# Two elementwise products of the finishing stage go from VectorE to Pool

## The reference

```
# attention: o per head (4 heads of 32), RMS norm per token and head, output product
o = o * rsqrt(mean(o * o, axis=-1) + 1e-5) * rms_w
o = o.reshape(B, L, 128) @ Wo
# feed-forward, 352 hidden columns, blocks of 16 rounded to FP4 with a scale each
gate = fp4_linear(x, w_gate);  y = fp4_linear(x, w_up)
h = silu(gate) * y
x + o + fp4_linear(h, w_down)
```

## Time and profile before

| | |
|---|---|
| median of 3 runs | 1819.68 us (1816.97 to 1820.57) |
| profiled execution | span 1818.1 us; no other time of it is shown |
| VectorE busy, share of the span | 1475.4 us, 81% |
| TensorE busy | 1450.2 us, 80% |
| ScalarE busy | 1025.9 us, 56% |
| Pool busy | 20.0 us, 1% |
| finishing pass | from 1553.3 us to the end, 16 tiles |

### The profile page before, as it was taken

The page is one execution under the profiler, slowest core; times in us unless marked ns, Lnnn a source line. Parts: engine busy times, 40 slices in busy tenths (PEclk is TensorE's granted clock), DMA queues, the critical chain, the costliest instruction groups (busy, mean ns, idle before and its releaser), DMA issues. The chain is left out here.

```text
span 1818.1 us, 38591 instructions
## 1 busy us (share of the span) xinstructions
PE 1450.2 (80%) x13559; PEld 1057.3 (58%) x13559; DVE 1475.4 (81%) x3537; ACT 1025.9 (56%) x1764; POOL 20.0 (1%) x41
## 2 busy tenths in 40 slices
PE   1569989999999999999977878724666567677776
PEld 0546666666666666666655666513555555466665
DVE  6785139888888888888877999859888887599996
ACT  0564348777777777777766777601111111577774
POOL 3000000000000000000000000000000000000000
PEclk9779999999999999999998899965556655788887
DMA  7000000000000000000001222250332210111111
GB/s 210 0 0 1 1 0 1 1 1 1 0 0 0 0 0 0 0 0 0 1 1 41 87 103 99 87 151 6 91 86 62 62 50 16 49 54 53 53 49 33
DMA packets 80860, 65.76 MB, mean 36 GB/s; under 512 B 3680, under 2 KB 65504, under 8 KB 80736
## 3 DMA queue, kind: packets, MB, share of 16 engines
q1 hardware_dynamic: 70128, 58.26, 10.3%
q10 hardware_dynamic: 10608, 5.79, 1.1%
HBM read 34.68 MB, written 29.36 MB: 35 GB/s over the span
## 5 line engine op out<-in xcount | busy, mean ns | idle before, releaser
L911 ACT ACTIVATE glu_a<-moe_a,b1s 128x512 f32<-128x512 f32 x256 | 176.7, 690 | 130.6 <-PE moe_a L822 128.3
L916 ACT ACTIVATE b_raw<-moe_b,b1s 128x512 f32<-128x512 f32 x256 | 176.3, 689 | 0.7 <-PE moe_b L822 0.5
L968 DVE TENSOR_TENSOR glu_a<-glu_a,moe_g 128x512 f32<-128x512 f32 x256 | 175.8, 687 | 0.0
L975 DVE TENSOR_TENSOR h_lo<-glu_a,h_hi 128x512 fp32r<-128x512 f32 x256 | 175.3, 685 | 0.6 <-ACT h_hi L927 0.6
L960 DVE SCALAR_TENSOR_TENSOR glu_a<-glu_a,b_raw 128x512 f32<-128x512 f32 x256 | 175.3, 685 | 0.1
L927 ACT ACTIVATE h_hi<-glu_a 128x512 fp32r<-128x512 f32 x256 | 161.8, 632 | 18.6 <-DVE glu_a L968 3.2
L951 DVE TENSOR_SCALAR b_raw<-b_raw 128x512 f32<-128x512 f32 x256 | 108.9, 425 | 72.9 <-ACT b_raw L916 72.9
L820 PE MATMUL moe_a<-x_hi,w_hi 128*128 128x512 f32 x256 | 127.2, 497 | 2.8 <-DVE w_lo L987 2.8
L849 PE MATMUL moe_y<-h_hi,w_hi 128*128 128x512 f32 x256 | 102.0, 399 | 2.7 <-DVE h_lo L975 2.7
L820 PE MATMUL moe_b<-x_hi,w_hi 128*128 128x512 f32 x256 | 101.7, 397 | 0.0
L821 PE MATMUL moe_a<-x_lo,w_hi 128*128 128x512 f32 x256 | 101.2, 395 | 0.0
(11 more groups left out here) (269 smaller groups left out, 3304.5 us busy)
## 6 DMA issues: line engine op xcount, KB each, us to landing
kq_scratch<-kq_out SPq DMA_DIRECT2D x16, 512.0 KB, 3.2
kq_in<-kq_scratch SPq DMA_DIRECT2D x16, 512.0 KB, 5.0
acc<-in_L_attn_inputs SPq DMA_DIRECT2D x8, 512.0 KB, 10.1
xq_scratch<-qT SPq DMA_DIRECT2D x16, 256.0 KB, 2.0
v_scratch<-v_out SPq DMA_DIRECT2D x16, 256.0 KB, 2.0
k_scratch<-k_out SPq DMA_DIRECT2D x16, 256.0 KB, 2.3
k_in<-k_scratch SPq DMA_DIRECT2D x8, 512.0 KB, 7.7
v_in<-v_scratch SPq DMA_DIRECT2D x8, 512.0 KB, 7.5
```

Of the source, the lines that this page charges most:

```text
L911: act.activation(glu_a[e % 4][:, :], ps_a[u][:, :], ACT.Gelu_apprx_sigmoid, bias=w["b1"][:, 0, e:e + 1]).then_inc(a_glu, 1)
L916: act.activation(b_raw[u][:, :], ps_b[u][:, :], ACT.Identity, bias=w["b1"][:, 1, e:e + 1])\
L968: dve.tensor_tensor(a, a, ps_g[u][:, :], ALU.mult).then_inc(weighted, 1)
L975: dve.tensor_tensor(h_lo[e % 2][:, :], glu_a[e % 4][:, :], h_hi[e % 2][:, :], ALU.subtract)\
```

## The change

`join` and `divide_o` are issued by Pool instead of VectorE, in a sweep of Pool's own, with the same operands. A new semaphore `divided` counts the second. VectorE's chain semaphore `o_chain` counts two steps per tile instead of three. In VectorE's list `back_o` moves from ahead of the first `add_h` to behind the second.

```diff
--- before.py
+++ after.py
@@ -1712,7 +1712,7 @@
         h_scaled, h_sized, h_over, c_set = sem("h_scaled"), sem("h_sized"), sem("h_over_ready"), sem("c_set")
         h_chain, h_ready, h_turned, h_copied = sem("h_chain"), sem("h_ready"), sem("h_turned"), sem("h_copied")
         down, final, stored = sem("ffn_down"), sem("final"), [sem(f"fin_stored{i}") for i in range(2)]
-        round_chain = sem("h_round_chain")
+        round_chain, divided = sem("h_round_chain"), sem("o_divided")
         acc = w["acc"]
 
         def half(a, h):
@@ -1726,6 +1726,21 @@
             @block.gpsimd
             def _(pool):
                 pool.memset(minus_c[:, :], -FP4_SHIFT * FP4_ONE).then_inc(c_set, 1)
+
+                def join(t, u):
+                    wait_free(pool, h_turned, t, 3)
+                    pool.wait_ge(silued, SUBS * (t + 1))
+                    pool.wait_ge(up_copied, SUBS * (t + 1))
+                    pool.tensor_tensor(hid[u][:, :, :], gated[u][:, :, :], lifted[u][:, :, :], ALU.mult)\
+                        .then_inc(joined, 1)
+
+                def divide_o(t, u):
+                    pool.wait_ge(o_chain, 2 * t + 2)
+                    r = rows[:, :].rearrange("p (n d) -> p n d", d=HD)
+                    pool.tensor_tensor(r, r, inv[:, :].unsqueeze(2).to_broadcast([P, NT, HD]), ALU.mult)\
+                        .then_inc(divided, 1)
+
+                sweep(pool, TILES, [(1, join), (1, divide_o)])
 
             @block.sync
             def _(sp):
@@ -1838,32 +1853,17 @@
 
                 def mean_o(t, u):
 
-                    dve.wait_ge(o_chain, 3 * t + 1)
+                    dve.wait_ge(o_chain, 2 * t + 1)
                     dve.tensor_scalar(m2[:, :], m2[:, :], 1.0 / HD, EPS, ALU.mult, ALU.add).then_inc(m2_ready, 1)
 
                 def invert_o(t, u):
                     dve.wait_ge(rooted, t + 1)
                     dve.reciprocal(inv[:, :], root[:, :]).then_inc(o_chain, 1)
 
-                def divide_o(t, u):
-                    dve.wait_ge(o_chain, 3 * t + 2)
-                    r = rows[:, :].rearrange("p (n d) -> p n d", d=HD)
-                    dve.tensor_tensor(r, r, inv[:, :].unsqueeze(2).to_broadcast([P, NT, HD]), ALU.mult)\
-                       .then_inc(o_chain, 1)
-
                 def back_o(t, u):
-                    dve.wait_ge(o_chain, 3 * t + 3)
+                    dve.wait_ge(divided, t + 1)
                     wait_free(dve, down, t, 1)
                     dve.transpose(oN[u][:, :], rows[:, :]).then_inc(o_ready, 1)
-
-                def join(t, u):
-                    wait_free(dve, h_turned, t, 3)
-                    dve.wait_ge(silued, SUBS * (t + 1))
-                    dve.wait_ge(up_copied, SUBS * (t + 1))
-                    dve.tensor_tensor(hid[u][:, :, :], gated[u][:, :, :], lifted[u][:, :, :], ALU.mult)\
-                       .then_inc(joined, 1)
-
-
 
                 groups = "p j (g k) -> p j g k"
                 spread = lambda a, h: a.rearrange("p (j g) -> p j g", j=SUBS)[:, 2 * h:2 * h + 2, :].unsqueeze(3)\
@@ -1927,9 +1927,9 @@
                                       ALU.add).then_inc(final, 1)
 
 
-                sweep(dve, TILES, [(1, turn_o), (1, join), (1, sum_o), (1, max_h), (1, mean_o), (1, scale_h),
+                sweep(dve, TILES, [(1, turn_o), (1, sum_o), (1, max_h), (1, mean_o), (1, scale_h),
                                    (1, invert_h), (1, divide_h(0)), (1, divide_h(1)), (1, negate_h),
-                                   (1, invert_o), (1, divide_o), (1, back_o), (1, add_h(0)), (2, finish), (1, add_h(1)),
+                                   (1, invert_o), (1, add_h(0)), (2, finish), (1, add_h(1)), (1, back_o),
                                    (1, subtract_h(0)), (1, subtract_h(1)), (1, multiply_h(0)), (1, multiply_h(1))])
```

## The result

The changed kernel takes 1875.78 us (median of 4 runs, 1873.71 to 1876.34) against 1820.12 us for the kernel before: 55.7 us more, ratio 1.0302 with a 95% interval of 1.0288 to 1.0317. It is slower, as forecast, but by five times the 10.9 us of the sum. The time is near that of rival A (1883 us), which had a chance of 0.32.

The account below looks back on a forecast made before the run. The prediction took the chain from multiply_h through TensorE, ScalarE and the second h_over to VectorE as the bound. It summed 10.1 + 1.3 - 0.5 = +10.9 us on 1819.7 to 1831 us (own range 1824 to 1836); full range 1824 to 1888.

Parts of the forecast that it names:

- the sum: Whole kernel: back_o 10.1, first tile 1.3, less 0.5 for join leaving VectorE, +10.9 us in all.
- rival A: VectorE's burst ending the step: Pool's join shuts out two-tile instructions, 3.5 us a step, 1883 us; chance 0.32.
- The chain bounds the step, VectorE's total doesn't: Each step: multiply_h, transposes, ScalarE, second h_over take 11.09 us, then VectorE alone 4.10 us.
- back_o on the chain, 16 x 0.63 = 10.1 us: Between second add_h and first subtract_h: back_o costs 0.63 us at each of 16 tiles, at most 11.4 in all.
- divide_o, gain 0: Ahead of VectorE's wait for h_over: its 0.69 us only lengthens the wait; on Pool 0.7, 1.3 or 2.1 us.
- First tile, +1.3: First tile, where ScalarE waits for mean_o: a join of 3.5 us on Pool delays max_h, +1.3 us.
- join leaves VectorE, gain 0.5 us: Start of step: mean_o comes 0.7 us earlier, but the root rarely waited for it; 0.5 us gained over the stage.
- So join may take 15.82 + 3.08 - 13.03 = 5.87 us at no price: From last lifted to next step's max_h: a join on Pool up to 5.87 us long costs nothing.
- All three are hidden: Pool's join at each estimated length, 1.58, 3.5 or 5.7 us, fits its room, the top by 0.2 us only.
- Rival B: VectorE's burst keeps Pool's join out until the step's end; max_h 0.5 us late, 1838 us; chance 0.18.
- Slower, 0.89: Whole kernel: chance of being slower by more than about 4 us, mostly needing only back_o on the chain.
- The steps of before lie between 14.8 and 15.4: Steps of the kernel before, in us; cited for TensorE's clock perhaps moving the forecast by 2 us.

Follow-up runs that it names:

- a1: Kernel before with only back_o moved behind the second add_h, join and divide_o staying on VectorE: 1831.88 us against 1821.95.
- a4: Changed kernel with one more wait, so Pool's join starts only when the tile before is multiplied: 1837.48 us, +15.5 against the kernel before.
- a3: Kernel before with only join moved to Pool: 1869.14 us, ratio 1.0268.
- c1: Kernel before with VectorE's order alone changed and each store a step later, nothing on Pool: 1812.70 us against 1820.16.
- c3: c1 with invert_o ahead of scale_h and TensorE's turn_h in two halves: 1804.53 us against 1820.16 for the kernel before.
- a2: Kernel before with only divide_o moved to Pool, back_o in its old place: 1822.60 us, ratio 1.0009.
- c2: c3 with divide_o on Pool, released by invert_o: 1801.66 us against 1820.16 for the kernel before.
- c4: c2 with the first half of join on Pool too, released when the tile before is multiplied: 1796.91 us against 1820.16 for the kernel before.
- b2: Kernel before plus, per tile on Pool, a 128x1408 copy behind a one-element-a-row product, nothing waiting for it: 1838.69 us against 1820.88.

## Why the prediction was wrong, point by point

- *The chain bounds the step, VectorE's total doesn't*: right. a1 moves one instruction and pays 9.9 us; the wait for h_over swallowed what left VectorE (41.2 us of it after, 40 predicted).
- *back_o on the chain, 16 x 0.63 = 10.1 us*: right, 9.9 in a1.
- *divide_o, gain 0*: right, +0.65 with an interval across zero; its length of 1.05 us lay between the bounds.
- *First tile, +1.3*: 1.1.
- *join leaves VectorE, gain 0.5 us*: no run isolates it; it is within the noise.
- *"So join may take 15.82 + 3.08 - 13.03 = 5.87 us at no price", and "All three are hidden"*: this step failed. It asked only who waits for join, and by that measure it was right (a4 shows the room: a max_h that starts 0.3 us beyond it costs 0.3). It left out what no row of before shows: that Pool's instruction, while it reads SBUF, holds off a VectorE instruction with two inputs in SBUF. The term was put at 0 and measured 3.04 us a step, +47.2 us in a3. It stood in rival A with the right place (the burst behind the second add_h), the right condition and a price of 3.5 us a step, against 3.04. I gave it 0.32 because no row showed Pool reading beside a two-tile instruction. But no row excluded it either. The absence of such a row was no evidence for a price of 0, and the timing, the worst possible, was known.
- *Rival B* (Pool is kept out until the burst ends): false. Pool came in at the first boundary between two VectorE instructions, in the middle of the burst.
- *The range, 1824 to 1888*: 1875.78 lies in it only because rival A had been taken into it. The forecast's own range ended at 1836. *Slower, 0.89*: back_o alone makes the kernel slower by an amount clear of noise, so the direction rested on a mechanism that holds; five sixths of the loss came from the one that was left out of the sum.
- *"The steps of before lie between 14.8 and 15.4"*: two of them are 14.74 us. Nothing hangs on it.

## What to carry to other kernels

Before an operation is moved to Pool, look at what VectorE does at the time when its inputs are complete. If VectorE's instructions there read two SBUF tiles and lie on the chain, they are late by nearly the length of Pool's instruction (here 2.95 us for 3.16), though no semaphore says so. Release it where VectorE waits or reads one tile (a4: one wait, some 40 us). And VectorE, busy for 94% of a step, wasn't the step's bound, since it waited for ScalarE in every step. First find what the engine has to do behind such a wait, and shorten that (c1, c3). Moving divide_o away was worth nothing before that (a2) and 0.19 us a step after it (c2).

## What the runs showed of the hardware

- A Pool instruction that reads SBUF (products and a copy, float32) and a VectorE instruction that reads two SBUF tiles (products, subtract_h) didn't run together; a product of 128x1408 costs VectorE 2.95 us, one of 128x704 1.46, a copy of 128x1408 1.15, a memset of 128x1408 (1.27 us) nothing. VectorE's transpose of one tile and its reduce keep their lengths beside Pool's product (0.71 and 0.69 us in a4), and so does a sum of one SBUF tile and one in PSUM (0.65 in c4).
- In a burst of VectorE instructions without a gap Pool got in at the next boundary or the one after it, and VectorE's following instruction waited: in the changed kernel in each of the 15 tiles that have such a burst beside join.
- The wait appears in no list of waits. It is hidden in lengths: subtract_h 3.839 us instead of 0.885, join 3.777 instead of 3.155, a product of one element a row 0.95 us in b2, with 0.24 at its shortest. "Busy" of both engines includes it, which is how VectorE's busy time rose by 9 us with 36.3 us of work taken off it.
- A product on Pool takes 2.2 ns an element here (3155 ns for 1408); a copy 1.0 (1352 ns at its shortest). The copy held VectorE for 1.15 us and the product for 2.95, so it is two and a half times as cheap, where the prediction's estimate by reads gave a factor of two.

The Trainium skill's figure (GPSIMD Engine Reference, 3.1, Elementwise), which the page gives for an add of 2048 elements, gives 3.1 and 1.1 us for join and divide_o, an estimate by length. Undisturbed the two products measured 3.155 and 1.05.
